# Two mixtures of experts in one kernel: gathered blocks turned 9 for 8 items instead of 3 for 2, in a ring of 16 places instead of 8

## The reference

```python
x = x + L0_conv(_ln_c(x))                       # linear attention with 5x5 convolutions
t = t + L0_ffn(_ln_t(t))                        # 8 experts, top 2, width 512, gelu
x = x + L1_conv(_ln_c(x))                       # softmax attention, per image
t = t + L1_ffn(_ln_t(t))                        # 16 experts, top 2, width 256, silu gate

# L0_ffn, for every expert e of 8
hdn = jax.nn.gelu(flat @ w1[e] + b1[e])
out = out + combine[:, e:e + 1] * (hdn @ w2[e] + b2[e])
# L1_ffn, for every expert of 16
hid = jax.nn.silu(x @ wg) * (x @ wu)
acc = acc + ce[:, None] * (hid @ wd)
```

## Time and profile before

| what | us |
|---|---|
| median of the three timed runs | 469.87 |
| lowest and highest of them | 469.56, 471.03 |
| the profiled execution, as a whole | 473.52 |
| its span, from first to last instruction | 471.8 |
| gathers of mixture 0, first start to last start | 157.57 to 206.92 |
| last scatter of mixture 0 starts | 264.48 |
| gathers of mixture 1, first start to last start | 349.11 to 396.73 |
| last scatter of mixture 1 starts | 453.13 |

### The profile page before, as it was taken

One profiled execution on the slowest core, in us unless ns is written; L12 is line 12 of the kernel. 1 busy time (PEld: TensorE's weight loads), 2 busy tenths in 40 slices (PEclk: granted clock), 3 DMA queues, 4 the chain that ended last, 5 costly groups with the idle time before them and its releaser, 6 DMA issues.

```text
span 471.8 us, 7850 instructions
## 1 busy us (share of the span) xinstructions
PE 376.3 (80%) x2497; PEld 316.2 (67%) x2497; DVE 234.2 (50%) x547; ACT 213.5 (45%) x549; POOL 196.1 (42%) x209
## 2 busy tenths in 40 slices
PE   6999999999574758985999399898466778878813
PEld 4667999998352548974999255675335767878812
DVE  2559665633347415643677284475752333434415
ACT  3256223333437425643566173473642455655403
POOL 9419993430002555665455300000237454555630
PEclk9599999999997677996899787999857799999965
DMA  5014446433653265911011340000031111111136
GB/s 146 0 21 81 101 92 90 69 44 40 214 149 102 61 179 167 305 48 46 23 41 35 101 107 0 1 0 1 18 88 52 34 42 37 36 41 40 40 109 186
DMA packets 44014, 35.26 MB, mean 75 GB/s; under 512 B 3800, under 2 KB 39752, under 8 KB 43976
## 3 DMA queue, kind: packets, MB, share of 16 engines
q1 hardware_dynamic: 36412, 24.70, 20.2%
q0 software_dynamic: 4096, 8.40, 6.0%
q10 hardware_dynamic: 3468, 1.67, 2.2%
HBM read 21.12 MB, written 7.34 MB: 60 GB/s over the span
## 4 chain that ended last, share of the span: by engine, by line
PE 68%; DVE 8%; issue 6%; ACT 6%; DMA 5%; another core or an unknown queue 3%; ACTq 1%; SPq 1%; POOL 1%; POOLq 0%; DVEq 0%
PE bank L1452 18%; PE bank L1473 12%; PE bank L1363 10%; PE bank L1214 2%; DMA ln_sq<-y 2%; PE bank L1462 2%; PE bank L1313 2%; PE bank L1499 2%; ACT w_block L721 2%; PE bank L1397 2%; PE bank L1232 2%; PE bank L1298 2%; PE bank L1540 1%; PE bank L1239 1%
## 5 line engine op out<-in xcount | busy, mean ns | idle before, releaser
L1452 PE MATMUL bank<-x_cols,w_block 128*128 x688 | 103.2, 298 | 23.1 <-ACT w_block L721 8.9
L1452 PEld LDWEIGHTS bank<-x_cols,w_block 128*128 128x128 f32 x688 | 92.5, 209 | 29.3 <-issue 29.1
L534 POOL DMA_INDIRECT x_rows<-tok,token x64 | 61.4, 960 | 66.1 <-DVE dest L1004 28.6
L541 POOL DMA_INDIRECT y<-wide,dest x64 | 62.3, 974 | 51.7 <-DVE wide L1086 41.3
L1473 PE MATMUL bank<-w_down,h_cols 128*128 x500 | 73.9, 286 | 2.7 <-DVE wide L1086 1.8
L1473 PEld LDWEIGHTS bank<-w_down,h_cols 128*128 128x128 f32 x500 | 66.0, 201 | 4.0 <-issue 3.7
L1363 PE MATMUL bank<-cmap,cw 128*128 128x112 f32 (+2 forms) x480 | 57.5, 275 | 0.0
L1363 PEld LDWEIGHTS bank<-cmap,cw 128*128 128x128 f32 x480 | 55.8, 192 | 1.5 <-issue 1.4
L721 ACT ACTIVATE w_block<-w_up 128x512 f32 x86 | 53.6, 624 | 1.1 <-issue 0.6
L324 POOL TENSOR_TENSOR cw<-pw_in,dw_band 128x640 f32<-128x640 f32 x24 | 39.3, 1661 | 32.0 <-ACT pw_in L606 17.0
L528 POOL MEMSET wide<- 128x4096 f32 x2 | 7.0, 3512 | 106.9 <-DVE xs L1137 64.3
(11 more groups left out here) (213 smaller groups left out, 583.6 us busy)
## 6 DMA issues: line engine op xcount, KB each, us to landing
cmap<-heads SPq DMA_DIRECT2D x48, 64.0 KB
w_up<-in_L_ffn_w_dram SPq DMA_DIRECT2D x1, 2048.0 KB, 8.6
tok<-ln_sq SPq DMA_DIRECT2D x8, 256.0 KB, 2.4
w_up<-in_L_ffn_gate_w_dram SPq DMA_DIRECT2D x4, 512.0 KB
w_up<-in_L_ffn_up_w_dram SPq DMA_DIRECT2D x4, 512.0 KB
w_down<-in_L_ffn_down_w_dram SPq DMA_DIRECT2D x4, 512.0 KB
wide<-y SPq DMA_DIRECT2D x8, 256.0 KB, 4.6
ln_sq<-y SPq DMA_DIRECT2D x8, 256.0 KB, 5.2
```

The lines of the kernel that those rows point to most:

```text
L534: pool.indirect_dma_start(out=x_rows[:, j % RING, :], out_offset=None, in_=tok_dram[r], in_offset=bass.IndirectOffsetOnAxis(ap=token[r][:, ...
L541: pool.indirect_dma_start(out=y_dram[r], in_=y_acc[:, s * C:(s + 1) * C], in_offset=None, out_offset=bass.IndirectOffsetOnAxis(ap=dest[r][ ...
L1452: mm = pe.matmul(bank[2 + j % 2][:, i * 128:(i + 1) * 128], w_block[:, j % 3, i * 128:(i + 1) * 128], x_cols[:, bass.ds(at[j], 128)], star ...
```

## The change

Three edits. The ring has 16 places instead of 8, so `x_rows` grows from 4 to 8 KB of each partition and POOL waits for a turn from the 17th gather on. The table of turns becomes 1 + 9n/8 in place of 1 + 3n/2. And the semaphores of the gathers are 16 shared ones instead of 8 for each mixture; mixture 1 waits for counts that go on from where mixture 0 left them.

```diff
-RING = 8
+RING = 16
...
 def turned_by(n):
-    return min(NB, 1 + 3 * n // 2)
+    return min(NB, 1 + 9 * n // 8)
...
+        gathered = [sem(f"gathered{i}") for i in range(RING)]
+
         class Moe:
             def __init__(m, n):
-                m.gathered = [sem(f"m{n}_gathered{i}") for i in range(RING)]
...
                     pool.indirect_dma_start(
                         out=x_rows[:, j % RING, :], out_offset=None, in_=tok_dram[r],
                         in_offset=bass.IndirectOffsetOnAxis(ap=token[r][:, j:j + 1], axis=0))\
-                        .then_inc(m.gathered[j % RING], 16)
+                        .then_inc(gathered[j % RING], 16)
...
-                        pe.wait_ge(m.gathered[k % RING], 16 * (k // RING) + 16)
+                        pe.wait_ge(gathered[k % RING], 16 * ((r * NB + k) // RING) + 16)
```

## The result

The changed kernel takes 476.15 us (median of 4 runs, 475.26 to 477.27) and the kernel before, beside it, 469.72. The ratio is 1.0143, with a 95% interval of 1.0097 to 1.0188: slower, by some 6 us. I had forecast 463.5 us and a gain. The profiled execution of the changed kernel took 476.78 us with a span of 475.0, 3.2 us longer than the span of before.

The account below looks back on a forecast made before the run. Bursts of POOL's indirect DMAs, with late news from TensorE, slow the mixtures' early stages. Gains of 7.0 us in mixture 0 and 0.4 in mixture 1, less 1.0, make 6.4: 463.5 us from 469.87, range 447 to 480.

Parts of the forecast that it names:

- What bounds the kernel: Item loops of both mixtures: slow stages go with bursts of POOL's indirect DMAs, TensorE's news coming some 1.8 us late.
- The ring, landing: Waits for gathers that haven't landed: 16 places gain at most 1.6 us in the whole program.
- The ring, the longer first row: First two stages of both mixtures become one burst of 25 gathers; the second takes 15 us for 4 items.
- The middle of the loop: Gathers mostly come singly, so items take 1.99 us in mixture 0 and 1.81 in mixture 1, against 2.4 before.
- The burst that doesn't end: Slower rival, steps 8 to 14: bursts and late news feed each other; 14.8 us for four items, 478 us; chance 0.31.
- The end of the gathers: Mixture 0: 25th gather by about 189, last near 200 instead of 207, last scatter near 257 instead of 264.
- The scatters: After mixture 0's gathers: 5 scatters in a burst, not 8; the slow stage holds 3 items (11.4 us), not 5.
- Just in time: Mixture 1, steps 3 to 7: blocks turned right before their item, 0.2 us later each; five items lose 1.0 us.
- The sum: Mixture 0 98.5 us against 105.5; mixture 1 102.6 against 103.0, less 1.0; together a gain of 6.4 us.
- mixture 1 as long as before within 2 us: Sign that the forecast is right: mixture 1's loop keeps its earlier length of 103.0 us to within 2 us.
- The rival by the page: Slow stages: products run longer than drawn, as TensorE's own work, so nothing changes; 470 us, chance 0.12.

Follow-up runs that it names:

- turns-only run: Kernel before with only the new table, 9 turns for 8, ring still 8: 471.1 us (1.003) on a chip at 470, 427.1 us (0.992) on another.
- fourth group: Runs on one chip where the kernel before took 430.7 us; the unaltered changed kernel took 424.6 us there, ratio 0.995.
- the record's runs: The runs of the main result: the changed kernel 476.15 us against 469.72 for the kernel before, ratio 1.0143.
- the second group: Old and new ring and table in all four combinations on one chip: kernel before 468.9 us, changed kernel 476.6 us, ratio 1.014.

## Why the prediction was wrong

**What bounds the kernel.** Right, for chips like the recorded one: the slow stages go with rows of POOL's DMAs and news that comes late. What I called my reading is now supported from two sides, by the longer row of gathers and by the row of 14 scatters. It is not the whole cause: on another chip the same rows do no harm. How a row makes news late is not shown.

**The ring, landing.** Right. The waits for a gather were 1.6 us before and are 1.3 now.

**The ring, the longer first row: this step failed.** I had seen that the first two stages would be one row, and took "the same 15 us for 4 items" for it in both mixtures. They hold 10 and 14 records, 1.3 and 1.8 items, and the row ended after 20 and 21 gathers and not 25, as the news of the fifth turn, in mixture 1 of the sixth, came late. The mistake was to price a longer row by the pace of a stage in which the old row had been broken: in the earlier trace rows POOL pauses after its 12th gather, until 173.45, and from there to 188.5 it started 7 more in place of the 12 of an unbroken row. In the whole row a single hand-over, from the drawn end of the first down product to its reader, took 14.0 us, where the broken one had 6.6, and TensorE stood for 10.91 us at a stretch. At my own 1.99 and 1.81 us an item, the 2.75 and 2.25 missing items are 9.5 us. The granted clock of that stage, 0.61 and 0.54 where it had been 0.77, is inside this loss; an up product there is drawn as 2.07 us in place of 1.06, and its share isn't told apart.

**The middle of the loop.** Right in its mechanism: from the 21st on the gathers mostly come alone, and the stages have 9.1 items in 19.5 us and 9.5 in 16.7, that is 2.1 and 1.8 us an item for the forecast 1.99 and 1.81. The burst that doesn't end, my slow rival, did not come about where I had put it, in steps 8 to 14: no copy waits 2 us for a turn there. Its time, 478, was near the measured 476, for another reason; that is luck.

**The end of the gathers.** Wrong as a consequence: the 25th gather by 189 and the last near 200 expected, 195.33 and 208.18 measured. The last scatter started at 265.14 and not near 257. The 16th turn came late because the first stages had so few items.

**The scatters.** Nearly right: 6 in a row for 5, in place of 8. By my paces the stage from 208 on would have held 6.8 items in its 19 us; it held 7. The turns-only run shows how much hangs on this: gathers that end late leave a heap, and a heap is a row.

**Just in time.** Right in kind, too small. It can be read where nothing else is late, in the changed kernel on the fourth group's chip, mixture 1, the up products of two items in the first eight and of two behind:

```profile
343.75 1.15 PE L1453 MATMUL bank<-x_cols,w_block 128*128 x8
...
345.52 1.15 PE L1453 MATMUL bank<-x_cols,w_block 128*128 x8
...
350.61 1.06 PE L1453 MATMUL bank<-x_cols,w_block 128*128 x8
...
352.06 1.06 PE L1453 MATMUL bank<-x_cols,w_block 128*128 x8
```

1.77 us an item against 1.45, so 0.32 us an item where I had said 0.2, and 1.6 us for five where I had 1.0. It lies within my bounds of 0 and 0.6.

**The sum.** I had mixture 0 at -7.0 and mixture 1 at +0.6. From first gather to last scatter they are +0.5 and +3.7. The miss is 7.5 and 3.1 us, and by this estimate the 9.5 us of the failed step with 0.6 of just in time make up 10.1 of its 10.6. On the scale of the medians I missed by 12.7 us, 476.15 for 463.5. The other 2 us aren't in the loops: I had set the profiled execution 3.65 us above the median, as before's was, and the changed kernel's was 0.6 above, which makes 3.0, while the rest of the program was 0.9 shorter. Of the signs that I had named, mixture 1 as long as before within 2 us failed too.

**The rival by the page.** The Trainium skill, "Perfetto Trace Analysis", section "Tensor Engine Instruction", says that the ends of products are computed. If TensorE's products simply ran longer than drawn, as its own work, a longer row of POOL's DMAs would not lengthen the stall, and the same kernel would not do 63 records in 15 us on another chip. Nor did TensorE sit in the product whose news was late: the first down product starts at 166.12, and before its news came at 181.14 TensorE had started an up product (171.67), a turn (173.53) and the next down product (173.75). As I had put it, that rival falls. What these runs can't tell apart is whether, on the chips at 470, the row of DMAs holds back TensorE's semaphores or the products' own completion: the records show either as late news.

## What to carry to other kernels

A deeper ring is not free because its buffers are: it lets the issuing engine run on without a pause, and what that engine's row does to others has to be priced at its full length, not by a stage in which the row was broken. When a limit on run-ahead is lifted, look for who profited from the pauses. And when a gain or loss rests on an effect whose cause isn't known, run both kernels on more than one chip: here the same change is a loss of 1.4% in the record's runs and in those of the second group, and none on the chip of the fourth.

## What the runs showed that I had not expected

The same kernel before took 468.9 to 469.7 us in the record's runs and in the second group, and 425.5 to 431.7 us in the other five groups, each on a chip of its own. The traces differ in the mixtures alone: the two loops of the changed kernel take 215.1 us in the record's trace and 165.1 in the fourth group's, and all the rest 260.0 and 261.4. In like windows that is 10 records against 63. On the chips at 470 TensorE's news reaches the others late while POOL's indirect DMAs follow one another at 1.25 to 1.3 us, both for gathers and for scatters: from 150 us on, ScalarE, VectorE and GpSimd wait 10 to 16 times over 1.5 us for a releaser that the profile doesn't know in each of the six traces, 50 to 83 us in all. In the 14 traces of the other chips they never do. What differs between the chips no run here shows.

Where nothing is late, POOL can become what the mixtures end on. With a ring of 4 and with all gathers spaced, the row of scatters starts later and runs on for some 14 us after mixture 0's last up product (4.8 us in the changed kernel), and 0.5 us more for each gather took the changed kernel to 22 to 27 us above the kernel before. The changed kernel keeps POOL's row of gathers whole there, and has the lowest median of all, 424.6 us; but medians of different chips don't compare, and by ratio the turns alone (0.992) are no worse than both (0.995). No version was found that beats both kernels on chips at 470 us; there nothing tried was faster than the kernel before.
